# Centred weights in place of a channel shift in a convolution, attention and feed-forward kernel

## What is computed

```python
x = tpl_inv @ x                          # 128x128 inverse of (1 - circulant), over the channels
t = tokens(x)                            # [16, 1024, 128]: a row per pixel
t = t + attention(layernorm(t))          # causal linear attention, 8 heads of 16
z = layernorm(t)                         # over the 128 channels of a row
g = mean over the rows of (relu(z @ gfc1.T + b) @ gfc2.T + b2)     # 8 gates per image
W1m, b1m, W2m, b2m = base + sum over e of g[e] * task_vector[e]    # weights of each image
r = z + relu(z @ W1m.T + b1m) @ W2m.T + b2m
t = t + layernorm(r) * gain + bias
```

## Time and profile before

| what | value |
|---|---|
| median of 3 runs | 734.12 us (732.48 to 737.25) |
| the profiled execution | 735.35 us, its span 733.4 us |
| busy over the span | PE 93%, DVE 88%, ACT 86%, POOL 68% |
| mean granted TensorE clock | 0.983 of 2.4 GHz |
| DMA | 82.58 MB, mean 113 GB/s |

### The profile page before, as it was taken

One profiled execution on the slowest core, in us unless ns is written; L12 is line 12 of the kernel. 1 busy time (PEld: TensorE's weight loads), 2 busy tenths in 40 slices (PEclk: granted clock), 3 DMA queues, 4 the chain that ended last, 5 costly groups with the idle time before them and its releaser, 6 DMA issues. The chain is left out here.

```text
span 733.4 us, 39983 instructions
## 1 busy us (share of the span) xinstructions
PE 683.1 (93%) x13026; PEld 531.0 (72%) x13026; DVE 647.6 (88%) x2535; ACT 634.2 (86%) x1780; POOL 498.8 (68%) x911
## 2 busy tenths in 40 slices
PE   3898999999999999999999998889999998999993
PEld 2576777777777777777777776767777797777772
DVE  5689999999999999999999999667998977998983
ACT  3689999999999999999999998457888876888883
POOL 3669999999999999999999997301333312333333
PEclk9999999999999999999999999799999999999998
DMA  4547876666666666666666665210222211222222
GB/s 138 109 111 130 154 139 151 143 147 147 148 138 156 143 144 149 147 152 144 143 149 151 136 142 119 38 37 17 77 83 72 86 44 45 87 72 72 86 86 72
DMA packets 200294, 82.58 MB, mean 113 GB/s; under 512 B 174028, under 2 KB 187503, under 8 KB 200184
## 3 DMA queue, kind: packets, MB, share of 16 engines
q1 hardware_dynamic: 200248, 81.98, 47.7%
HBM read 22.69 MB, written 17.30 MB: 55 GB/s over the span
## 5 line engine op out<-in xcount | busy, mean ns | idle before, releaser
L900 DVE SCALAR_TENSOR_TENSOR scores_lo<-p_a,scores_hi 128x512 f16<-128x512 f32 x256 | 170.6, 677 | 1.2 <-ACT scores_hi L781 1.2
L781 ACT ACTIVATE scores_hi<-p_a 128x512 f16<-128x512 f32 x256 | 162.7, 646 | 4.9 <-PE p_a L617 4.8
L1433 POOL TENSOR_TENSOR ffn_rstd_shift<-ffn_rstd_shift,consts 128x4 f32<-128x4 f32 x32 | 36.8, 1150 | 110.9 <-DVE ffn_rstd_shift L1391 110.9
L1260 ACT ACTIVATE h_f<-psb,merged_b_of_batch 128x512 f32<-128x512 f32 x128 | 87.3, 712 | 11.7 <-PE psb L1196 10.1
L1215 PE MATMUL psb<-merged_W_of_batch,h_hi 128*128 128x128 f16 x512 | 94.5, 220 | 2.3 <-DVE h_lo L1369 1.6
L1369 DVE TENSOR_TENSOR h_lo<-h_f,h_hi 128x512 f16<-128x512 f32 x128 | 95.5, 785 | 1.3 <-ACT h_hi L1271 1.2
L1216 PE MATMUL psb<-merged_W_of_batch,h_hi 128*128 128x128 f16 x512 | 94.2, 220 | 0.0
L1217 PE MATMUL psb<-merged_W_of_batch,h_lo 128*128 128x128 f16 x512 | 94.2, 220 | 0.0
L634 PE MATMUL p_o<-v_parts,scores_hi 128*128 128x17 f16 x1024 | 90.4, 171 | 2.4 <-issue 0.6
L1001 POOL CAST qk_parts<-qk_f 128x512 f16<-128x512 f32 x128 | 78.3, 612 | 17.9 <-issue 15.7
L634 PEld LDWEIGHTS p_o<-v_parts,scores_hi 128*128 128x128 f16 x1024 | 81.6, 96 | 11.8 <-issue 9.2
(11 more groups left out here) (214 smaller groups left out, 2775.3 us busy)
## 6 DMA issues: line engine op xcount, KB each, us to landing
x_f<-in_x SPq DMA_DIRECT2D x32, 256.0 KB, 3.0
t_rows<-t SPq DMA_DIRECT2D x64, 128.0 KB, 2.0
t_back<-t_rows SPq DMA_DIRECT2D x32, 256.0 KB, 2.6
out<-out_tile SPq DMA_DIRECT2D x32, 256.0 KB, 2.0
tv_share<-in_L_ffn_tv_W SPq DMA_DIRECT2D x32, 128.0 KB, 2.2
qkT_parts<-qk_parts SPq DMA_TRANSPOSE x128, 3.1
zT_hi_lo<-z_parts SPq DMA_TRANSPOSE x64, 2.4
merged_W<-in_L_ffn_W SPq DMA_DIRECT2D x2, 256.0 KB, 4.3
```

The lines of the kernel that those rows point to most:

```text
L781: nc.scalar.activation(ah[:, t % 2, cols], p_a[:, cols], ACT.Relu).then_inc(ahi_ready[eo], 1)
L900: nc.vector.scalar_tensor_tensor(al[:, t % 2, cols], p_a[:, cols], 0.0, ah[:, t % 2, cols], ALU.max, ALU.subtract).then_inc(alo_ready[eo], 1)
L1260: nc.scalar.activation(hf_[:, c, :], ps[:, c, :], ACT.Relu, bias=b1s[:, h // 2, c:c + 1], scale=1.0 / WS).then_inc(h_ready[c], 1)
```

## The change

The product that makes t1 uses the inverse with its channel mean taken out (`pa[:, 1, 128:256]` in place of `pa[:, 1, 0:128]`) and W_out with its mean over the output channels taken out, so t1 comes without its mean. The mean itself is a 129th column of the weights (C1 = 129; the query, key and value columns begin at Q0 = 144). `yt`, the rows in memory and `t1b` have 129 columns. `shift2` and its semaphore are gone, and `normalise` is a copy with a scale and no bias. In the second phase a new POOL stage, `add_mean`, adds column 128 of `t1b` to the other 128 before `add_up` adds them to the result.

```diff
-                ("state_lo", 3), ("stats1", 0), ("tv_lo", 0), ("eps2", 8), ("shift2", 9), ("mean_var1", 0),
+                ("state_lo", 3), ("stats1", 0), ("tv_lo", 0), ("eps2", 8), ("mean_var1", 0),
...
-FFN_GPSIMD_ORDER = [("rsqrt", 2), ("gain", 2)]
+FFN_GPSIMD_ORDER = [("add_mean", 2), ("rsqrt", 2), ("gain", 2)]
...
-                    nc.vector.tensor_scalar(wbig[:, 0:C], pa[:, 1, 0:128], WSI, None, ALU.mult)
+                    nc.vector.tensor_scalar(wbig[:, 0:C], pa[:, 1, 128:256], WSI, None, ALU.mult)
+                    link(nc.vector.tensor_reduce(wom[:, 2:3], pa[:, 1, 0:128], AX.X, ALU.add))
+                    nc.vector.tensor_scalar(wbig[:, C:Q0], wom[:, 2:3].broadcast_to([P, Q0 - C]), WSI / C, None, ALU.mult)
...
-                    nc.vector.tensor_scalar(woT[:, :], wsqT[:, 3, :], WSI, None, ALU.mult)
+                    link(nc.vector.tensor_reduce(wom[:, 0:1], wsqT[:, 3, :], AX.X, ALU.add))
+                    link(nc.vector.tensor_scalar(wom[:, 1:2], wom[:, 0:1], 1.0 / C, None, ALU.mult))
+                    nc.vector.tensor_scalar(woT[:, 0:C], wsqT[:, 3, :], wom[:, 1:2], WSI, ALU.subtract, ALU.mult)
+                    nc.vector.tensor_scalar(woT[:, C:C1], wom[:, 1:2], WSI, None, ALU.mult)
...
-                        o, cols = p_m1[:, 0:P], slice(j * P, (j + 1) * P)
-                        mm(o, xh[:, hf, cols], wh[:, 0:C], start=True, stop=False)
-                        mm(o, xh[:, hf, cols], wl[:, 0:C], start=False, stop=False)
-                        mm(o, xl[:, hf, cols], wh[:, 0:C], start=False, stop=False)
+                        o, cols = p_m1[:, 0:C1], slice(j * P, (j + 1) * P)
+                        mm(o, xh[:, hf, cols], wh[:, 0:C1], start=True, stop=False)
+                        mm(o, xh[:, hf, cols], wl[:, 0:C1], start=False, stop=False)
+                        mm(o, xl[:, hf, cols], wh[:, 0:C1], start=False, stop=False)
...
-                        nc.scalar.activation(yt[:, t, :], p_m1[:, 0:P], ACT.Copy, scale=1.0 / WSI).then_inc(t1_ready, 1)
+                        nc.scalar.activation(yt[:, t, :], p_m1[:, 0:C1], ACT.Copy, scale=1.0 / WSI).then_inc(t1_ready, 1)
...
-                        act.wait_ge(shift_ready, n + 1)
+                        act.wait_ge(rstd2, n + 1)
                         at_least(act, zlo_ready, n - 1)
-                        nc.scalar.activation(z_[:, t % 2, :], yt[:, t, :], ACT.Identity, bias=st2[:, t % 4, 10:11],
-                                             scale=st2[:, t % 4, 8:9]).then_inc(z_ready, 1)
+                        nc.scalar.activation(z_[:, t % 2, :], yt[:, t, 0:C], ACT.Copy, scale=st2[:, t % 4, 8:9])\
+                            .then_inc(z_ready, 1)
...
-                        dve.wait_ge(t1_loaded[hf], 16 * (2 * pair + h // 2 + 1))
-                        nc.vector.tensor_tensor(rn[:, hf, :, :], rn[:, hf, :, :], t1b[:, hf, :, :], ALU.add)\
+                        dve.wait_ge(raised, q + 1)
+                        nc.vector.tensor_tensor(rn[:, hf, :, :], rn[:, hf, :, :], t1b[:, hf, :, 0:C], ALU.add)\
                             .then_inc(v_ready, 1)
...
+                    def add_mean(g, pair, h):
+                        q, hf = HB * pair + h, h % 2
+                        pool.wait_ge(t1_loaded[hf], 16 * (2 * pair + h // 2 + 1))
+                        nc.gpsimd.tensor_tensor(t1b[:, hf, :, 0:C], t1b[:, hf, :, 0:C],
+                                                t1b[:, hf, :, C:C1].broadcast_to([P, HALF, C]), ALU.add)\
+                            .then_inc(raised, 1)
```

More of the change, by code:

```diff
@@ L36 @@
 TVW = FO * C // B
+C1 = C + 1
+Q0 = C + 16
 PKW = 2 * (NH * 4 * DH + DH)
@@ L133, in build @@
         delta2h = sb(top, "delta2_f16", [P, GB, FI], F16)
-        wh = sb(top, "w_in_hi", [P, 4 * C], F16)
-        wl = sb(top, "w_in_lo", [P, 4 * C], F16)
-        woT = sb(top, "w_outT", [P, C])
+        wh = sb(top, "w_in_hi", [P, Q0 + 3 * C], F16)
+        wl = sb(top, "w_in_lo", [P, Q0 + 3 * C], F16)
+        woT = sb(top, "w_outT", [P, C1])
         gfh = sb(top, "gate1_hi", [P, C], F16)
@@ L205, in build @@
             vp = sb(early, "v_parts", [P, 8, NH, 2 * DH + 1], F16)
-            yt = sb(early, "t1", [P, TILES, C])
+            yt = sb(early, "centred_t1_and_mean", [P, TILES, C1])
             g2n = sb(early, "gate2_rows", [E, C])
@@ L215, in build @@
             casd = sb(su, "cas_scaled", [P, 2, C])
-            wbig = sb(su, "w_in", [P, 4 * C])
+            wbig = sb(su, "w_in", [P, Q0 + 3 * C])
+            wom = sb(su, "w_out_mean", [P, 3])
             cw = sb(su, "centred_inverse", [P, C])
@@ L304, in _ @@
                     dve.wait_ge(s_pch, 3)
-                    nc.vector.tensor_scalar(wbig[:, C:3 * C], pa[:, 4, 0:2 * C], WSI, None, ALU.mult)
-                    link(nc.vector.tensor_scalar(wbig[:, 3 * C:4 * C], pa[:, 4, 2 * C:3 * C], WSI * VS, None, ALU.mult))
+                    nc.vector.tensor_scalar(wbig[:, Q0:Q0 + 2 * C], pa[:, 4, 0:2 * C], WSI, None, ALU.mult)
+                    link(nc.vector.tensor_scalar(wbig[:, Q0 + 2 * C:Q0 + 3 * C], pa[:, 4, 2 * C:3 * C], WSI * VS, None, ALU.mult))
                     link(nc.vector.tensor_copy(wh[:, :], wbig[:, :]))
@@ L395, in build @@
              av_done, den2, o_ready, ot_done, oT_ready, wo_done,
-             t1_ready, bn2, mv2, ve2, rstd2, shift_ready, z_ready, zhi_ready, zlo_ready, gt_done, gate_ready) = [
+             t1_ready, bn2, mv2, ve2, rstd2, z_ready, zhi_ready, zlo_ready, gt_done, gate_ready) = [
                 sem(s) for s in (
@@ L569, in project @@
                         cols = slice(j * P, (j + 1) * P)
-                        mm(p_in[:, t % 2, 0:3 * C], xh[:, hf, cols], wh[:, C:4 * C], start=True, stop=False)
-                        mm(p_in[:, t % 2, 0:3 * C], xh[:, hf, cols], wl[:, C:4 * C], start=False, stop=False)
-                        mm(p_in[:, t % 2, 0:3 * C], xl[:, hf, cols], wh[:, C:4 * C], start=False, stop=True).then_inc(in_done, 1)
+                        mm(p_in[:, t % 2, 0:3 * C], xh[:, hf, cols], wh[:, Q0:Q0 + 3 * C], start=True, stop=False)
+                        mm(p_in[:, t % 2, 0:3 * C], xh[:, hf, cols], wl[:, Q0:Q0 + 3 * C], start=False, stop=False)
+                        mm(p_in[:, t % 2, 0:3 * C], xl[:, hf, cols], wh[:, Q0:Q0 + 3 * C], start=False, stop=True).then_inc(in_done, 1)
                     def state(b, t):
@@ L878, in make_qk @@
                                                        ALU.min, ALU.add).then_inc(qk_ready, 1)
[L880 to L884, removed]
                     def state_lo(b, t):
@@ L920, in stats2 @@
                         dve.wait_ge(t1_ready, n + 1)
-                        nc.vector.bn_stats(st2[:, t % 4, 0:6], yt[:, t, :]).then_inc(bn2, 1)
+                        nc.vector.bn_stats(st2[:, t % 4, 0:6], yt[:, t, 0:C]).then_inc(bn2, 1)
                     def mean_var2(b, t):
@@ L965, in _ @@
                     run(dve, VECTOR_ORDER, {"tv_lo": tv_lo, "stats1": stats1, "mean_var1": mean_var1, "v_lo": v_lo,
-                        "make_qk": make_qk, "shift2": shift2, "state_lo": state_lo,
+                        "make_qk": make_qk, "state_lo": state_lo,
                         "scores_lo_0": scores_lo(0), "scores_lo_1": scores_lo(1),
@@ L1052, in build @@
             hl = sb(pb, "h_lo", [P, 2, FC, 512], F16)
-            t1b = sb(pb, "t1_back", [P, 2, HALF, C])
+            t1b = sb(pb, "t1_back", [P, 2, HALF, C1])
             rn = sb(pb, "normed", [P, 2, HALF, C])
@@ L1061, in build @@
             (b1_ready, gs_ready, g_done, g9r, b12_done, b_chain, gb_ready,
-             w2_copied, f2_done, fbn, fmv, fve, frs, fsh, n_ready, gain_ready, v_ready,
+             w2_copied, f2_done, fbn, fmv, fve, frs, fsh, n_ready, raised, gain_ready, v_ready,
              t_done, ob_ready) = [sem(s) for s in (
                 "b1_ready gs_ready g_done g9_ready b12_done b_chain gb_ready "
-                "w2_copied f2_done fbn fmv fve frs fsh n_ready gain_ready v_ready "
+                "w2_copied f2_done fbn fmv fve frs fsh n_ready raised gain_ready v_ready "
                 "t_done ob_ready").split()]
@@ L1437, in _ @@
                     nc.gpsimd.memset(ob[:, 1, :], 0.0).then_inc(out_stored[1], 16)
-                    run(pool, FFN_GPSIMD_ORDER, {"rsqrt": rsqrt, "gain": gain})
+                    run(pool, FFN_GPSIMD_ORDER, {"rsqrt": rsqrt, "gain": gain, "add_mean": add_mean})
 _INS = ["x", "L0_conv_width", "L0_conv_damp", "L1_attn_W_q", "L1_attn_W_k", "L1_attn_W_v", "L1_attn_W_out",
@@ L1462 @@
         aps[name[3:]] = nc.dram_tensor(name, a.shape, mybir.dt.from_np(a.dtype), kind="ExternalInput").ap()
-    aps["t1"] = nc.dram_tensor("t1_rows", (NHALF * P, HALF * C), F32, kind="Internal").ap()
+    aps["t1"] = nc.dram_tensor("t1_rows", (NHALF * P, HALF * C1), F32, kind="Internal").ap()
     aps["base_parts"] = nc.dram_tensor("base_parts", (2, 2, P, BW), F16, kind="Internal").ap()
```

4 lines of the change are left out of this document (2 added, 2 removed).

## The result

The changed kernel takes 753.62 us in the median of six executions, 752.39 without one of 1963 us that lies far from all others; the kernel before beside it takes 734.63 us. The ratio, without that one, is 1.0242, its 95% interval 1.0201 to 1.0282: 2.4% slower. The profiled execution took 755.52 us, its span 753.6 us, against 735.35 and 733.4 before. The difference of the spans, 20.2 us, splits at two marks. The first convolution product starts at 17.59 us in place of 16.50, 1.09 later; the first product of the merging behind the first phase at 475.01 in place of 479.89, 4.88 earlier. So the setup costs 1.09, the first phase gains 4.88 + 1.09 = 5.97, and what follows loses 20.2 + 4.88 = 25.1 us.

What follows compares the result with a forecast made beforehand. It took ACT, then PE, to bound the first phase and DVE's loop the second. 1.0 - 5.8 + 0.3 + 34.2 = +29.7 us on 735.35 gave 765.0, or 764 us against the median; range 747 to 778.

Steps and rivals of the forecast that it cites:

- add_mean's price: Second phase: DVE's two-SBUF-operand instructions lose 1.14 us a slot to add_mean behind gain, over 30 slots +34.2 us.
- -5.8 + 0.3: First phase: z without bias operand on ACT saves 5.8 us; PE's products with one more column cost 0.3.
- I cost it at nothing; ACT's pace hides it: First phase: removing shift2 from DVE, 26.0 us by lengths over 128, gains nothing, as DVE waits for ACT anyway.
- The rule of one z per pair of slots: First phase: ACT passes z twice per pair, but only one saving of 0.09 us counts: 64 x 0.09 = 5.8 us.
- Setup: Before the first phase: added row sums, scaling, strip and column on DVE's chain cost +1.0 us (0.5 to 1.5).
- Load: Second phase: t1's wider load lands in 2.6 us, with 2.2 us of slack before add_mean can begin.
- Nobody disturbed: Second phase: add_mean delays no engine, so the kernel gets faster, 729.6 or 724 us; chance 0.10.
- POOL kept waiting: Second phase: DVE's instructions hold add_mean back, making rsqrt 0.70 us late a slot, 751 us; chance 0.15.
- The clock: Second phase: TensorE's clock falls in each slot as PE waits longer for h_lo, another 11 us, 775; chance 0.12.

Runs made afterwards that it cites:

- the half-sized run: The changed kernel with add_mean over only 64 of the 128 channels of each row: 740.41 us, ratio 1.0105.
- the power of 4 elements: The changed kernel with add_mean replaced, at the same place on POOL, by a power reading 4 elements a row: 726.72 us, ratio 0.9920.

## Why the prediction came out as it did

*Direction and mechanism.* Right: add_mean in POOL's idle time stops DVE's h_lo, DVE's loop has no pause for it, and the second phase loses several times what the first gains. Without add_mean the kernel is faster, with it slower, and a POOL instruction as long that streams hardly anything costs nothing. Only the order was told otherwise: the first h_lo gets through and holds add_mean for 0.45 us, and the second then pays alone. The time lies within the range of 747 to 778, 10 to 12 us below the forecast of 764.

*The step that was mis-sized* is add_mean's price, "30 x 1.14 = +34.2 us". The thirty slots were right, the price was 0.84. It took add_mean for as long as gain, 1.27, while alone it takes 1.04 us; and it took nearly the whole length for streaming, where 0.2 us of it are not (the half-sized run: 0.617 long, 0.42 lost). 30 x 0.30 = 9 us, nearly all of the 9.5 between the +29.7 forecast for the profiled execution and its 20.2.

*First phase.* -5.8 + 0.3 was forecast, -5.97 came, but the attribution failed. "I cost it at nothing; ACT's pace hides it" was said of DVE's shift2: with z's cheaper form alone the phase gains 2.0 us by its pace, and only the whole change, with shift2 gone, 6. The rule of one z per pair of slots gave the right number by chance. Its evidence was misread as well: of the 7.4 us that the earlier trace rows puts down to PE's gate product 7.2 lie at 456 to 479 us, where the phase runs out. That ACT waits there at full pace too is shown by its starts alone, 0.49 us against 0.36, and that this wait gets longer came true. The view that should have warned was the one that the prediction began with: DVE 97.49 beside ACT 99.52 leaves 2 us in 100 until DVE leads, and z's 0.09 of 3.35 us a tile are 2.7 in 100.

*Setup.* +1.0 forecast, +1.09 in the profiled execution; in the eight other traces with the same setup the first product comes 0.6 to 1.0 us after the 16.50 of before. *Load.* t1's load still lands in 2.6 us, and only the first add_mean waits for it.

*The rivals.* Nobody disturbed: no, 0.84 us a slot is above its 0.39. POOL kept waiting: its time (751) is near, its mechanism isn't what happened. POOL is held, for 0.45 us, but rsqrt keeps 1.72 us of idle time ahead of it. The clock: 1.00 between 620 and 712, although PE waits about 1 us a slot. (The 6.4 us of PE's work in that rival stand in no row; by its busy time they are about 6.55 a slot, which would add some 4 us to that rival's 775.)

The Trainium skill (SBUF — State Buffer, Who interferes with whom) says that whichever of the two engines issues first keeps the shared ports for the whole instruction. Both orders are seen in one slot here, POOL holding the second h_lo and the first h_lo holding POOL. For the whole instruction the runs don't agree: 0.84 of add_mean's 1.04 us hold DVE, and the power of 4 elements, 1.01 us long, holds it not at all.

## What to carry to other kernels

Idle time on POOL was not free for streaming work with DVE in the loop and two SBUF operands in its instructions: price it at its streaming time on whatever such instruction of DVE comes next, however small that is. Look first for an engine with a wait of its own, and fill that wait to less than its length (0.88 us of 0.94 was hidden, 1.19 not quite). Where several engines stand within 2% of each other, take the gain of a change from all its edits together, since here each edit alone gave less than its share (2.0 and 1.1 of 6.0 us).

## What was not expected of the hardware

A POOL addition with an operand of one element a row, repeated, took 1.04 us for 512 elements, gain's multiplication by a row 1.27; which of operation and operand does it wasn't tried. A DVE instruction on 4 elements a row can take 0.99 us in place of 0.16, and a POOL instruction on 4 elements 1.46 in place of 1.01, when the other engine streams.
